# A gated delta-rule attention layer with a mixture-of-experts layer behind it: x loaded in groups, output weights waited for late, and a new order of the work inside a head step

## The reference, cut to what matters

```python
x = x + attention(layernorm(x))      # 8 heads of 128
x = x + moe(layernorm(x))            # 8 experts, top 2, and a shared one

# attention, for each sequence and head:
q, k, v = silu(conv4(x @ Wq.T)), silu(conv4(x @ Wk.T)), silu(conv4(x @ Wv.T))
q, k = rms-normalised and scaled
g = -exp(A_log) * softplus(x @ Wfa.T @ Wfb.T + dt_bias)
beta = sigmoid(x @ Wb.T)
for t in range(512):                 # a 128 x 128 state S for each head
    S = S * exp(g[t])[..., None]
    S = S + k[t] (x) (beta[t] * (v[t] - k[t] @ S))
    o[t] = q[t] @ S
out = (rms(o) * o_norm_w * sigmoid(x @ Wga.T @ Wgb.T)) @ Wo.T
```

## Time and profile before

| what | value |
|---|---|
| median of three runs | 5362.73 us |
| time of the profiled execution | 5360.98 us |
| its span, first to last instruction | 5359.2 us |
| mean granted TensorE clock | 0.976 |
| PE, DVE, ACT, POOL busy | 93%, 70%, 61%, 54% |
| start to PE's first instruction | 71.3 us |
| 128 head steps and their three last | to about 4533 us |
| mixture of experts | about 4544 us to the end |

### The profile page before, as it was taken

How to read it: one execution, slowest core, us unless ns; L and a number is a source line. 1 busy time by engine, 2 the same in 40 slices (tenths; PEclk the granted TensorE clock), 3 DMA queues, 4 the chain that set the end, 5 groups by cost and what they waited for, 6 DMA issues and landing times.

```text
span 5359.2 us, 114813 instructions
## 1 busy us (share of the span) xinstructions
PE 4957.4 (93%) x30720; PEld 3937.7 (73%) x30720; DVE 3775.5 (70%) x8897; ACT 3289.2 (61%) x7088; POOL 2882.2 (54%) x6210
## 2 busy tenths in 40 slices
PE   3999999999999999999999999999999997999999
PEld 2778787877787878787878777777777786555555
DVE  2777777777777878686877777786777784555555
ACT  2767676767676767676777767676777673111111
POOL 1766666666575757666666656666666673000000
PEclk9999999999999999999999999999999997999999
DMA  2111111111111111111111111111111111000000
GB/s 89 35 31 40 29 38 31 38 33 36 35 35 31 39 29 37 31 37 33 35 36 35 36 31 36 33 36 33 36 35 36 33 37 38 8 12 8 12 12 12
DMA packets 214188, 173.47 MB, mean 32 GB/s; under 512 B 146432, under 2 KB 164096, under 8 KB 213376
## 3 DMA queue, kind: packets, MB, share of 16 engines
q1 hardware_dynamic: 213504, 165.49, 10.9%
HBM read 119.03 MB, written 46.40 MB: 31 GB/s over the span
## 4 chain that ended last, share of the span: by engine, by line
PE 72%; issue 10%; POOL 7%; ACT 4%; DVE 3%; DMA 3%; POOLq 1%; SPq 0%; DVEq 0%; ACTq 0%
PE bank L1346 12%; PE bank L1559 9%; PE bank L1257 9%; PE bank L1368 6%; PE bank L1312 5%; PE bank L1569 4%; PE bank L1327 4%; PE bank L1394 3%; POOL rm L399 2%; POOL mul L395 2%; PE bank L1271 2%; PE bank L1409 2%; PE bank L1265 2%; DMA lx<-blocks_in 2%; PE bank L1381 2%
## 5 line engine op out<-in xcount | busy, mean ns | idle before, releaser
L376 POOL TENSOR_TENSOR kl<-kl,tot 128x256 f32<-128x256 f32 x768 | 502.1, 654 | 820.0 <-PE bank L1346 634.7
L1346 PE MATMUL bank<-kq,kl 128*128 128x128 f32 x6144 | 858.4, 282 | 71.1 <-DVE kq L854 45.0
L1346 PEld LDWEIGHTS bank<-kq,kl 128*128 128x128 f32 x6144 | 750.6, 192 | 122.5 <-issue 86.9
L1257 PE MATMUL bank<-xT,par 128*128 128x512 f32 x1536 | 771.7, 599 | 6.2 <-DVE xall L981 5.8
L399 POOL TENSOR_TENSOR rm<-rm,mul 32x14 f32<-32x14 f32 (+6 forms) x1792 | 579.1, 323 | 140.3
L395 POOL TENSOR_TENSOR mul<-pm,rm 32x14 f32<-32x14 f32 (+6 forms) x1792 | 516.4, 288 | 136.3 <-issue 36.4
L854 DVE TENSOR_TENSOR kq<-kq,tot 128x512 f32<-128x512 f32 x768 | 533.2, 694 | 0.0
L981 DVE TENSOR_TENSOR xall<-xall,bank 128x512 f32 (+1 forms) x256 | 175.7, 687 | 413.5 <-PE bank L1327 411.9
L864 DVE COPY_PREDICATED AT<-mask,bank 128x256 f32<-128x256 uint32 x896 | 466.4, 521 | 0.0
L838 DVE COPY_PREDICATED lx<-mask,bank 128x256 f32<-128x256 uint32 x512 | 296.4, 579 | 213.7 <-PE bank L1346 213.6
L356 POOL TENSOR_TENSOR rstd<-rstd,minus_half 128x4 f32<-128x4 f32 x32 | 32.3, 1008 | 739.1 <-DVE rstd L801 739.1
(11 more groups left out here) (173 smaller groups left out, 12854.0 us busy)
## 6 DMA issues: line engine op xcount, KB each, us to landing
par<-params_dram SPq DMA_DIRECT2D x128, 519.0 KB, 3.5
blocks_out<-lx SPq DMA_DIRECT2D x128, 256.0 KB, 2.0
lx<-blocks_in SPq DMA_DIRECT2D x128, 256.0 KB, 2.8
xall<-x_dram SPq DMA_DIRECT2D x16, 512.0 KB, 3.8
pm<-blocks_out SPq DMA_DIRECT2D x512, 8.0 KB
blocks_in<-rm SPq DMA_DIRECT2D x512, 8.0 KB
out_dram<-xall SPq DMA_DIRECT2D x16, 512.0 KB, 2.9
lx<-ffn_dram SPq DMA_DIRECT2D x1, 3456.0 KB, 11.0
```

The lines of the kernel that those rows point to most:

```text
L376: pool.tensor_tensor(halves(kl[:, :], w)[:, :, 0, :], src, totr.broadcast_to([P, SEQ // (2 * w), w]), ALU.mult).then_inc(s["kl_ready"], 1)
L1257: ins = pe.matmul(bank[t][:, :], par[p][:, at:at + P], chunk(xT, kt, SEQ), start=kt == 0, stop=kt == KT - 1)
L1346: ins = pe.matmul(dst[:, :, n], chunk(left, n), right[:, :, n, :, 1, :], start=True, stop=True)
```

## The change

The first load brings sequence 0 alone. The 15 others come in five groups of three, one issued by SP at the head of each of steps 0 to 4; `next_moments` waits for all of them. PE waits for the output weights in step 3, where `project_out` first reads them. `next_params` stands before `blocks_to_pool`. All five lists of calls have a new order. PE waits in the first three steps (without stage C) for DVE's `l_evict` before it writes the level bank again, and DVE's `kq_update` names its level there.

```diff
-            for b in range(BATCH):
-                sp.dma_start(xall[:, b * NCH * HID:(b + 1) * NCH * HID].rearrange("p (n d) -> p n d", d=HID),
-                             xt[:, b * NCH:(b + 1) * NCH, :]).then_inc(s["x_in"], 16)
...
-                sp.wait_ge(s["x_in"], 16 * (b + 1))
...
+            load_x(0, 1)
...
+                    if isinstance(i, int) and i < XPARTS:
+                        sp.wait_ge(s["x_in"], 16 * (i + 1))
+                        load_x(1 + i * (BATCH - 1) // XPARTS, 1 + (i + 1) * (BATCH - 1) // XPARTS)
...
+                next_x()
                 if D:
                     blocks_from_pool()
                     diagonals_back()
                 if B:
                     low_levels_out()
+                    next_params()
                     blocks_to_pool()
-                    next_params()
...
-            pe.wait_ge(s["wo_in"], 16)
...
+                        if isinstance(i, int) and i == LAG:
+                            pe.wait_ge(s["wo_in"], 16)
...
+                    if not C:
+                        dve.wait_ge(s["lvl_mm"], LEVELS * iB + l + 1)
...
                 def next_moments():
...
-                        dve.wait_ge(s["x_in"], nb * 16 + 16)
+                        dve.wait_ge(s["x_in"], 16 * (1 + XPARTS))
...
+                next_moments()
                 if B:
                     l_evict(0)
+                    kq_update(0)
                     qk_evict(0)
+                if A:
+                    conv(0, 1)
                 if C:
                     s_update(0)
...
+                next_scale()
+                if B:
+                    qk_evict(6)
+                if A:
+                    scales()
+                    diagonal()
```

More of the change, by code:

```diff
@@ L473, in step @@
                     totals(5)
+                if B:
+                    kl_update(5)
+                    first_columns(iB)
+                if A:
                     totals(6)
                 if B:
-                    kl_update(5)
-                if A:
-                    totals(7)
+                    eliminate(iB, 1)
+                    eliminate(iB, 2)
                 if C:
                     norms()
[L481 to L488, removed]
                 if A:
@@ L722, in step @@
                 if C:
-                    output_squares()
+                    w_evict(3)
+                if N:
+                    fa_evict(nb)
+                if A:
+                    silu(0)
+                    silu(1)
+                    square(0)
+                    square(1)
                 if D:
@@ L726, in step @@
                     tt_evict(4)
-                if A:
-                    silu(0)
-                    silu(1)
+                if C:
+                    output_squares()
+                if N:
+                    ga_evict(nb)
                 if B:
@@ L732, in step @@
                 if A:
-                    square(0)
-                    square(1)
+                    silu(2)
                 if D:
@@ L740, in step @@
                 if A:
-                    silu(2)
                     gate()
                 if N:
-                    turned_x(nb, 0)
-                    turned_x(nb, 1)
-                    fa_evict(nb)
-                    ga_evict(nb)
                     beta_exp(nb)
@@ L1009, in step @@
                     l_evict(1)
-                if A:
-                    conv(1, 2)
+                    qk_evict(1)
+                if C:
+                    s_update(1)
                 if B:
-                    qk_evict(1)
                     kq_update(1)
@@ L1035, in step @@
                     qk_evict(3)
+                if A:
+                    conv(2, 1)
+                if B:
+                    l_evict(4)
                 if C:
@@ L1483, in step @@
                     lt_times_t(4)
+                if B:
+                    level(4)
+                if N:
+                    turn_next_x(nb, 1)
+                if C:
+                    k_times_s(3)
+                if A:
+                    project_g(3)
+                if D:
+                    t_products(4)
                 if C:
                     solve(3)
+                if N:
+                    next_fa(nb)
                 if B:
-                    level(4)
+                    level(5)
                 if C:
```

159 lines of the change are left out of this document (75 added, 84 removed).

## The result

The changed kernel takes **5197.38 us** (median of four runs, 5193.51 to 5205.7) against 5361.31 for the kernel before in the same comparison: a ratio of 0.9693, interval 0.9675 to 0.9711. It is 3.1% faster, 164 us. The forecast was 5078, 285 less, with a range from 5025 to 5175: the sign was right, the size not, and the time lies 22 us above the range.

What follows compares the result with a forecast made beforehand. PE, 93% busy, was taken as the bound, with waits at the start, in the turning step and in every step. Passes -213, first pass -13, last steps -2, start -57: -285, giving 5078 us, range 5025 to 5175.

Steps and rivals of the forecast that it cites:

- The start: Kernel start: PE's first instruction moves from 71.3 to about 14.6 us, -57 us, with the groups of x costing nothing.
- The rival that x or the weights stand in the way of the blocks: SP's DMA queue: weights hold the block reads, up to 5453 us, slower than before; 4 in 100. x groups: 55 at worst.
- The argument against that rival: SP's DMA queue: the 1.1 us in which the weights move already fall into the wait for the block write.
- The turning step: Turning step of each pass: spread parts find the bank emptied and run at full clock, 6.5 instead of 17.3 us, -10.8.
- The rival of 12 us: Turning step keeps its waits and low clock: 12 us instead of 6.5, 83 more in all, 5160 us; 12 in 100.
- The moments and the loop head: `next_moments` moves from DVE's tail to its head: 0.4 of 2.25 us left, 1.85 less a pass; loop-head cost of 2.7 stays.
- The ordinary step: Eight ordinary steps a pass: 31.3 us each, a gain of 0.3, with bounds 30.8 and 32.1.
- the layout of DVE's list: DVE in the ordinary step: operations laid out at the length of their old records; PE then waits 1.7 us, 31.0 in all.
- the two cycles over POOL, 31.1 and 31.3: Ordinary step: the cycle over the blocks closes in 31.1 us, the one over `norms` in 31.3, the last setting the step.
- The sign that was named for them: POOL in the ordinary step: `first_columns` started by the blocks' arrival and no longer behind `norms`.
- The 0.3 added for the weights ahead of the blocks: Blocks' cycle of the ordinary step: weights sent ahead of the four block reads add 0.3 us, 30.8 to 31.1.
- The first rival: Ordinary step gains nothing as waits of DVE's making grow: 32.1 us, 5178 us, covering 5130 to 5200; 17 in 100.

Runs made afterwards that it cites:

- the best version: Changed kernel with DVE's `outputs` moved ahead of `kq_init(0)` and `kq_init(1)` moved behind `qk_evict(5)`: 5075.89 us, 0.9481 of the kernel before.

## Why the prediction was wrong, point by point

**The start** was right: -57 forecast, 56.7 in PE's first instruction (71.34 to 14.68), 57.7 between the medians of the kernel that has only this and the one before. The groups of x, 7.0 us each, held back nothing. The rival that x or the weights stand in the way of the blocks fell with the two runs on it. The argument against that rival had a number wrong all the same: in the changed kernel the packets of the weights take 2.3 us (median), not 1.1, and run from 1.7 to 4.0 us after the write is issued, so that most of them fall behind the wait of 2.13 and not into it. Even so the last packet of the blocks comes 2.42 us after the reads are issued, against 2.34 in the kernel before.

**The turning step** was right in its size: 17.3 to 6.5 forecast, 17.2 to 6.3 found, though with a clock of 0.96 in the step shown and not 1.00. But its reason was too narrow. The kernel with the block put back shows that only 6.6 of the 10.9 us come from spreading the five parts; the rest comes with the surrounding order. The rival of 12 us did not come.

**The moments and the loop head.** The moments step lost 2.2 (1.85 forecast), and the loop head's excess was to stay and stayed, at 3.3 of mean value where one pass had shown 2.7. The statistics did move their cost there, and by the run that undoes the move the net gain is small: the sum came out right partly by luck, because the new order has a shorter loop head of its own (34.25 with the moments at the tail, 1.85 over its ordinary step, where it was 3.36 over before).

**The ordinary step** is where the prediction failed: "PE 31.0, blocks 31.1, norms 31.3. The last to close sets the step: 31.3". It is 32.37, 1.07 more. That makes 1.07 x 8 x 14 = 120 us, and 5197 - 120 = 5077 is the forecast but for one. The failed step is the layout of DVE's list, in which every instruction had the length of its record in the kernel before. `kq_init(1)` and `kq_init(0)` went in at 0.73 us each. In the new order they meet `first_columns` and `q_times_k` on POOL, and take 1.34 and 1.76. That brought two waits of PE, 0.35 at level 6 and 0.88 at `turn_og`, where the layout had none. The chain is shown at both ends: with POOL's product cut short the step is 31.45 and the time 5080, and with the two calls moved behind what PE waits for it is 31.23 and 5076.

The other waits of the layout came nearly as forecast (0.74 for 0.85 at `k_times_s(2)`, 0.41 for 0.4 at level 5, 0.19 for 0.15 at `state_update(2)`). Whether the two cycles over POOL, 31.1 and 31.3, were right no run shows: the step of 31.23 in the best version lies near them, but on its page POOL has 3% of the chain. The sign that was named for them, `first_columns` started by the arrival of the blocks, holds in 28 of 128 steps; in the step shown it follows the sixth `kl_update` at once. The 0.3 added for the weights ahead of the blocks has no counterpart either: with the weights behind them the step is 32.40. The step of the best version was not set by the wait at `k_times_s(2)` alone: taking that away changed nothing.

**The first rival**, that the ordinary step gains nothing because of waits of DVE's making, is the one that came, a little beyond its price (32.1, 5178) and inside the 5130 to 5200 that it was to cover. But it expected the three waits of the layout to grow; they did not, and two others came. I gave it 17 in 100, and its price was an upper bound of "0.8 of waits that I have not seen". A step longer than 32.1 was not among my bounds for this, though two instructions of DVE are enough for it. The place to look was in the order itself: which products of POOL stand beside which products of DVE. The other rivals, transfers in the way and a turning step that keeps its waits, did not come.

**The rule that bears on it.** The Trainium skill, page "SBUF — State Buffer", section "Who interferes with whom", says that a DVE instruction with two inputs in SBUF contends with a GpSimd instruction that reads SBUF, and that the order in which they are issued decides which one is held up. The traces agree: DVE's product, the later of the two, goes from 0.73 to 1.76 us and ends 0.55 after POOL's, while the products of DVE that begin first, `kq_update(5)` and `kq_update(6)`, keep 0.70 and 0.68, and POOL's behind them are the longer ones (`first_columns` 1.23 on average instead of 0.85, `q_times_k` 1.53 instead of 1.26). The prediction did not ask for this.

**What stays open.** The best version took 5076 where 5055 had been expected, and which cycle holds its step at 31.23 was not settled. What the engines do in the up to 2.5 us at the turn of the loop was not tried.

## What to carry to other kernels

When lists of work are reordered, the durations of the old trace hold only for instructions that keep their neighbours on the other engines: mark the products of two tiles on VectorE and on GpSimd, and check that none begins beside another where something waits behind it. Where a meeting can't be avoided, put the instruction that others wait for first and let the one whose result is needed late take the delay; here two such exchanges were worth 2.2% of the whole time. And an order of several engines is one object: a group moved on PE alone cost 7% here, since DVE's list had been written for its place.

## What the runs showed of the hardware

- A product of two 128 x 512 tiles on VectorE takes 0.68 to 0.73 us alone, 1.34 (median) when it begins during a product of two 32 x 256 tiles on GpSimd, and 1.76 during one of two 128 x 512 tiles. Its end came 0.55 to 0.56 us behind GpSimd's in all 235 such meetings in the trace of the changed kernel, and 0.55 when it began only 0.18 us ahead of GpSimd's end. So its length was set by how much of GpSimd's was left, as if it had waited for that; how the two share the time inside was not measured.
- The one that began first kept its length: 0.70 and 0.68 us on VectorE, with the product on GpSimd that began behind it at 1.25 and 1.55 instead of 0.85 and 1.26.
- At the turn of the hardware loop DVE and ACT stood still for 2.52 us that no semaphore explains, POOL for 1.67, PE for 1.37 (in the kernel before PE for 2.52). Work placed at the head of the loop, which looked free in an ordinary step, was added to this delay.
- TensorE's granted clock was 0.83 in the turning step of the kernel before, with its waits of 5.0 us in all, and 0.96 in that of the changed one. Fewer waits did not always mean less time at the lower level: over fourteen passes it was 55 us in the kernel with `outputs` first, which waits less than the changed one with its 24. With the parts in a block and one first wait of 1.00 us instead of 2.61, `next_fa` still ran at 1.2 GHz (3.67 us), but `next_ga` behind it at 2.4 GHz (1.98 against 3.78).
